# A macaron block on one core: other order of loads and first steps, scatters in four parts, gates by four 64 by 64 products, new places for the recurrence's work

## The reference

```python
x = x + 0.5 * ffn(layernorm(x))      # mixture of 8 experts, top 1
x = x + recurrence(layernorm(x))     # 3 layers over time, width 64
x = x + 0.5 * ffn(layernorm(x))      # same weights as the first

def ffn(x):                          # per token
    p = softmax(x @ Wr + br); e = argmax(p)
    h = relu(affine(layernorm(x)) @ W1[e] + b1[e])        # 256 -> 1024
    return (h @ W2[e] + b2[e]) * max(p)                   # 1024 -> 256

def layer(x):                        # width 64, x begins as h @ down_w.T
    xc = conv_b + sum(shifted(x, k) * conv_w[:, k] for k in range(4))
    r, i = sigmoid(xc @ Wr.T + br), sigmoid(xc @ Wi.T + bi)
    a = exp(8 * r * log_sigmoid(log_a))
    h[t] = a[t] * h[t - 1] + sqrt(1 - a * a)[t] * (i * xc)[t]
    return rms_norm(h @ out_w.T) * norm_w   # up_w takes it back to 256
```

## Time and profile before

| | |
|---|---|
| median of 3 runs | 768.86 us (766.00 to 772.32) |
| profiled execution, its own time | 763.67 us |
| its span, first to last instruction | 761.9 us |
| mean granted clock of TensorE | 0.930 |
| PE, DVE, ACT, POOL busy, share of the span | 90%, 54%, 35%, 23% |
| 16 DMA engines | 166 GB/s over the span |

### The profile page before, as it was taken

How to read it: one execution, slowest core, us unless ns; L and a number is a source line. 1 busy time by engine, 2 the same in 40 slices (tenths; PEclk the granted TensorE clock), 3 DMA queues, 4 the chain that set the end, 5 groups by cost and what they waited for, 6 DMA issues and landing times.

```text
span 761.9 us, 15311 instructions
## 1 busy us (share of the span) xinstructions
PE 684.7 (90%) x4350; PEld 594.2 (78%) x4350; DVE 410.7 (54%) x1427; ACT 264.3 (35%) x630; POOL 172.7 (23%) x178
## 2 busy tenths in 40 slices
PE   5548889899999999998997798989999889999993
PEld 4437679899988877887775686878888789999992
DVE  6466356333346576856877585865667332333331
ACT  3123112322334557343644454432522223222230
POOL 4622551111121120251212511240124111111111
PEclk9557899999999999999996898998999999999997
DMA  8989453665564444255253305353536464454440
GB/s 259 279 289 379 154 195 105 234 201 203 180 218 138 158 164 138 78 184 199 73 177 105 113 15 208 126 183 110 180 99 220 155 199 148 139 197 133 159 136 13
DMA packets 59919, 126.51 MB, mean 166 GB/s; under 512 B 8105, under 2 KB 36660, under 8 KB 59700
## 3 DMA queue, kind: packets, MB, share of 16 engines
q1 hardware_dynamic: 53204, 108.50, 43.7%
q0 software_dynamic: 6624, 16.92, 6.0%
HBM read 106.36 MB, written 20.35 MB: 166 GB/s over the span
## 4 chain that ended last, share of the span: by engine, by line
PE 80%; issue 6%; DVE 6%; ACT 2%; another core or an unknown queue 2%; DVEq 2%; DMA 1%; POOL 0%; SPq 0%; ACTq 0%; POOLq 0%
PE bank L1631 33%; PE bank L1645 33%; PE bank L1546 2%; PE bank L1618 2%; PE bank L1486 2%; PE bank L1551 1%; DVE st L717 1%; PE bank L1556 1%; PE bank L1538 1%; PE bank L1566 1%; PE bank L1577 1%; PE bank L1501 1%; PE bank L1514 1%; DMA rows<-in_L_attn_h 1%
## 5 line engine op out<-in xcount | busy, mean ns | idle before, releaser
L1645 PE MATMUL bank<-w,act_t 128*128 x1184 | 287.0, 393 | 9.3 <-issue 7.7
L1631 PE MATMUL bank<-mn_t,w 128*128 128x128 f32 x2368 | 287.3, 278 | 3.9 <-issue 3.9
L1631 PEld LDWEIGHTS bank<-mn_t,w 128*128 128x128 f32 x2368 | 278.7, 195 | 10.5 <-issue 10.2
L1645 PEld LDWEIGHTS bank<-w,act_t 128*128 128x128 f32 x1184 | 225.6, 197 | 48.9 <-issue 20.0
L1136 DVE TENSOR_SCALAR act_t<-bank,vec 128x128 f32<-128x128 f32 x296 | 83.5, 344 | 122.2 <-PE bank L1631 101.0
L1367 ACT ACTIVATE mn_t<-bank,vec 128x128 f32<-128x128 f32 x152 | 61.4, 454 | 230.3 <-PE bank L1618 215.2
L1377 ACT ACTIVATE act_t<-bank,vec 128x128 f32<-128x128 f32 x296 | 85.0, 368 | 105.8 <-PE bank L1631 76.5
L1143 DVE TENSOR_TENSOR y_b<-bank,b_all 128x256 f32<-128x256 f32 x74 | 31.4, 424 | 119.9 <-PE bank L1645 105.2
L625 POOL DMA_INDIRECT out_x<-res,pay x37 | 36.4, 984 | 243.4 <-DVE res L1149 242.8
L625 POOL DMA_INDIRECT x_middle<-res,pay x37 | 39.7, 1074 | 216.9 <-DVE res L1149 215.5
L616 POOL DMA_INDIRECT routed_rows<-rows,dest x64 | 63.5, 992 | 51.9 <-DVE dest L817 34.5
(11 more groups left out here) (211 smaller groups left out, 456.6 us busy)
## 6 DMA issues: line engine op xcount, KB each, us to landing
w<-in_L_ffn_W SPq DMA_DIRECT2D x82, 1024.0 KB
pay<-routed_rows SPq DMA_DIRECT2D x78, 130.0 KB, 2.1
rows<-in_L_attn_h SPq DMA_DIRECT2D x8, 512.0 KB, 6.9
rows<-x_middle SPq DMA_DIRECT2D x8, 512.0 KB, 5.1
routed_rows<-fill SPq DMA_DIRECT2D x2, 1040.0 KB, 10.7
b_all<-in_L_ffn_b SPq DMA_DIRECT2D x1, 1024.0 KB
routed_rows<-rows,dest POOLq DMA_INDIRECT x64
x_middle<-res,pay POOLq DMA_INDIRECT x37, 3.2
```

The source lines that it names most:

```text
L1631: last = t.matmul(b_hid[half][:, c % 4 * P:(c % 4 + 1) * P], w1[i % W1S][:, k * F + c * P:k * F + (c + 1) * P], mn_t[p][i % 2][:, k * P:(k ...
L1645: last = t.matmul(b_out[i % 2], act_t[i % 2][:, c * P:(c + 1) * P], w2[:, ds(eb * (WE // FC) + c * D, D)], start=c == 0, stop=c == FC - 1)
```

## The change

It does seven things. SP's queue: chunk 0, router weights, chunk 1, router bias, four `w2`, chunks 2 and 3, the parameters; after `s_tab` the first `w1`, a `w2` by use, the rows, and so on, and last the fill. The wait for the fill moves from the scatters to SP, ahead of the loads of the rows of the later parts. The first chunks' order on PE and ACT is changed: `ranks` of chunk 0 stands between the two transposes of chunk 1, and the exponentials between two keeps. `centre_down` goes ahead of the last table part, and the moments of chunk 3 go into slot 0. A chunk's 8 scatters stand at four positions, two at each, instead of two with four at each. The gates are four products of 64 by 64 weights, with one signal at the end: the input gate's go to bank 1 with the two sequences swapped, the other gate's to bank 0 unswapped, so that each of the four takes rows and columns of the array of its own; ACT's tanh of the input gate becomes two activations of 64 partitions that swap back. And nearly all positions are new. Cut to its core (the first hunk shows only the constants of which the text speaks):

```diff
@@ the positions (line 22 on) @@
...
-LN_TRANSPOSE = [[3984, 4032], [5065, 5089], [6576, 6624], [8065, 8089]]
...
-RESCALE = [[1009, 1278, 1681, 2065], [1152, 1416, 1827, 2260], [1275, 1608, 2040, 2424]]
-TAP = [[1034, 1279, 1705, 2065], [1176, 1416, 1922, 2281], [1276, 1610, 2041, 2426]]
-CONVOLVE = [[1032, 1296, 1705, 2112], [1153, 1464, 1829, 2280], [1277, 1632, 2042, 2472]]
-GATES = [[4224, 5232, 6960, 8544], [4776, 5952, 7680, 9264], [5160, 6625, 8256, 10032]]
...
-SCAN = [[1104, 1369, 1800, 2209], [1248, 1560, 1970, 2376], [1320, 1728, 2136, 2544]]
-PROJECT = [[4512, 5544, 7248, 9024], [5064, 6336, 8064, 9624], [5376, 7008, 8592, 10320]]
-SQUARES = [[1128, 1370, 1920, 2256], [1272, 1608, 2016, 2424], [1322, 1753, 2161, 2592]]
-NORMS = [[4560, 5569, 7250, 9072], [5088, 6384, 8088, 9672], [5424, 7104, 8640, 10368]]
...
-R_CHOOSE = [[None, None, 1, 120], [1417, 1872, 2304, 2736]]
...
-R_PLACE = [[None, None, 72, 192], [1488, 1969, 2352, 2784]]
...
-R_MOMENTS = [[1392, 1393], [1824, 1828], [2257, 2259], [2616, 2688]]
-R_SCATTER = [[[None, None], [None, None], [24, 25], [96, 97]], [[744, 745], [1008, 1009], [1176, 1177], [1392,
-    1393]]]
-TABLE_PARTS = [[[None, None, None, None, None, None], [217, 240, 264, 336, 337, None]], [[1514, 1609, 1658, 1659,
-    1660, 1704], [2041, 2064, 2066, 2067, 2137, 2138], [2400, 2425, 2473, 2474, 2475, 2520], [2809, 2832, 2833,
-    2834, 2835, None]]]
-LAYER_COLUMNS = 0
...
+LN_TRANSPOSE = [[3984, 4032], [5089, 5113], [6720, 6816], [8329, 8353]]
...
+RESCALE = [[1032, 1299, 1731, 2281], [1153, 1440, 1872, 2451], [1297, 1560, 2090, 2689]]
+TAP = [[1034, 1320, 1752, 2281], [1176, 1440, 1922, 2472], [1277, 1562, 2117, 2712]]
+CONVOLVE = [[1033, 1300, 1733, 2304], [1176, 1442, 1968, 2520], [1298, 1584, 2092, 2736]]
+GATES = [[4248, 5328, 7008, 9264], [4800, 5832, 7896, 10176], [5232, 6432, 8448, 11040]]
...
+SCAN = [[1104, 1392, 1800, 2400], [1248, 1512, 2064, 2592], [1416, 1728, 2208, 2808]]
+PROJECT = [[4560, 5664, 7248, 9720], [5088, 6144, 8328, 10488], [5713, 6913, 8904, 11328]]
+SQUARES = [[1128, 1416, 1920, 2424], [1272, 1536, 2112, 2640], [1418, 1753, 2232, 2832]]
+NORMS = [[4608, 5712, 7369, 9768], [5112, 6192, 8352, 10536], [5737, 7009, 9048, 11376]]
...
+R_CHOOSE = [[None, None, 48, 168], [1536, 1969, 2352, 2904]]
...
+R_PLACE = [[None, None, 72, 192], [1561, 2040, 2424, 2952]]
...
+R_MOMENTS = [[[None, None], [None, None], [None, None], [0, 1]], [[1464, 1489], [1824, 1825], [2305, 2306], [2857,
+    2880]]]
+R_SCATTER = [[[None, None, None, None], [None, None, None, None], [25, 48, 49, 72], [96, 97, 98, 120]], [[768, 792,
+    793, 794], [1008, 1032, 1033, 1034], [1200, 1224, 1225, 1226], [1464, 1488, 1489, 1490]]]
+TABLE_PARTS = [[[None, None, None, None, None, None], [217, 240, 312, 336, 337, None]], [[1608, 1632, 1730, 1732,
+    1734, 1752], [2066, 2089, 2091, 2093, 2094, 2112], [2450, 2472, 2473, 2474, 2521, 2544], [2977, 3000, 3001,
+    3002, 3003, None]]]
+LAYER_COLUMNS = 49
...
@@ -474,6 +476,9 @@
                     s = FIRST[p].index(i)
+                    if (p, s) != (0, 0):
+
+                        sp.wait_ge(s_fill[p], 16)
                     sp.wait_ge(s_tab, tables_at(p, s))
@@ -538,29 +543,29 @@
+            load_x(0, 0)
             sp.dma_start(wr[:, :].rearrange("p (k e) -> p k e", k=KD),
                          router_w.rearrange("(k p) e -> p k e", p=P)).then_inc(s_rt, 16)
-            sp.dma_start(rb_all[:, :], router_b[None, :].to_broadcast([P, E])).then_inc(s_rt, 16)
-            load_x(0, 0)
             load_x(0, 1)
-            sp.wait_ge(s_c2, 1)
-            empty_rows(0)
+            sp.dma_start(rb_all[:, :], router_b[None, :].to_broadcast([P, E])).then_inc(s_rb, 16)
+            for e in range(EAGER):
+                second_weights(e)
             load_x(0, 2)
-            second_weights(0)
+            load_x(0, 3)
             load_parameters()
-            load_x(0, 3)
-            for e in range(1, EAGER):
-                second_weights(e)
+
...
             slot_weights(0, 0)
+            sp.wait_ge(s_order, 1)
+            second_weights_by_use(0)
             for i in range(RING - 1):
                 next_rows(0, i)
-            sp.wait_ge(s_order, 1)
             for i in range(1, W1S):
-                second_weights_by_use(i - 1)
                 slot_weights(0, i)
-            for k in range(W1S - 1, LATER):
+                second_weights_by_use(i)
+            for k in range(W1S, LATER):
                 second_weights_by_use(k)
+            empty_rows(0)
...
@@ -607,12 +612,11 @@
-            def route(f, c, b):
+            def route(f, c, part):
...
                 pool.wait_ge(s_ds[f], c + 1)
-                pool.wait_ge(s_fill[f], 16)
-                for j in range(TPC):
-                    t = (b * NC + c) * TPC + j
+                for k in range(2 * part, 2 * part + 2):
+                    t = (k // TPC * NC + c) * TPC + k % TPC
                     g.indirect_dma_start(
@@ -636,9 +640,9 @@
                                 powers(m, c)
-                            for b in range(NB):
-                                if k == R_SCATTER[f][c][b]:
-                                    route(f, c, b)
+                            for part in range(NJ // 2):
+                                if k == R_SCATTER[f][c][part]:
+                                    route(f, c, part)
...
@@ -678,8 +682,8 @@
             for c in range(HC):
-                for b in range(NB):
-                    route(0, c, b)
+                for part in range(NJ // 2):
+                    route(0, c, part)
             first_pass()
@@ -743,7 +747,7 @@
             def centre_router():
-                dve.wait_ge(s_rt, 32)
+                dve.wait_ge(s_rt, 16)
                 dve.wait_ge(s_wrc, 1)
@@ -763,6 +767,7 @@
                     v.memset(seen, 0.0)
+                    dve.wait_ge(s_rb, 16)
                 m, rs = mv[0][cc], inv_std[0][cc]
@@ -1091,8 +1096,9 @@
                                 add_recurrence(c, part)
-                            if k == R_MOMENTS[c][part]:
-                                moments(R2, c, part)
+                            for f, m in ((0, R1), (1, R2)):
+                                if k == R_MOMENTS[f][c][part]:
+                                    moments(m, c, part)
                         if k == LN_WIDE[c]:
@@ -1236,11 +1242,10 @@
             order_of_use()
+            centre_down()
             tables(0, 0, 5)
-            centre_down()
-            for c in range(HC, NC):
-                for b in range(NB):
-                    moments(R1, c, b)
+            for b in range(NB):
+                moments(R1, 2, b)
             norm(0, 0)
@@ -1311,8 +1316,13 @@
                 cc = c % 2
-                act.wait_ge(r_g[c % 2], 2 * turn(l, c))
-                a.activation(r_ti_b[cc], bk[cc][1][:, :], ACT.Tanh, scale=0.5, bias=unit(l, U_IB)).then_inc(r_t[c % 2], 1)
+                act.wait_ge(r_g[c % 2], turn(l, c))
+                for b in range(NB):
+
+                    o = NB - 1 - b
+                    last = a.activation(r_ti_b[cc][b * DO:(b + 1) * DO, :], bk[cc][1][o * DO:(o + 1) * DO, :], ACT.Tanh,
+                                        scale=0.5, bias=unit(l, U_IB)[o * DO:(o + 1) * DO, :])
+                last.then_inc(r_t[c % 2], 1)
                 a.activation(r_a_b[cc], bk[cc][0][:, :], ACT.Tanh, scale=0.5, bias=unit(l, U_RB))
@@ -1428,13 +1438,13 @@
             keep_logits(R1, 0)
-            for part in range(2):
-                keep(R1, 1, part)
+            keep(R1, 1, 0)
             exponentials(0, 0)
+            keep(R1, 1, 1)
             keep_logits(R1, 1)
-            for part in range(2):
-                keep(R1, 2, part)
+            keep(R1, 2, 0)
             exponentials(0, 1)
+            keep(R1, 2, 1)
             keep_logits(R1, 2)
@@ -1487,7 +1497,7 @@
             def router_sums():
-                pe.wait_ge(s_rt, 32)
+                pe.wait_ge(s_rt, 16)
                 for k in range(KD):
@@ -1540,10 +1550,14 @@
                 pe.wait_ge(r_xc[c % 2], turn(l, c))
-                for m in range(2):
-                    o = (m * NL + l) * P
-                    t.matmul(bk[c % 2][m][:, :], rec_t[:, o:o + P], r_x_b[c % 2], start=True, stop=True).then_inc(r_g[c % 2], 1)
+                for m, b in ((1, 0), (1, 1), (0, 0), (0, 1)):
+                    o = (m * NL + l) * P + b * DO
+                    to = (b + m) % NB
+                    last = t.matmul(bk[c % 2][m][to * DO:(to + 1) * DO, :], rec_t[b * DO:(b + 1) * DO, o:o + DO],
+                                    r_x_b[c % 2][b * DO:(b + 1) * DO, :], start=True, stop=True)
+                last.then_inc(r_g[c % 2], 1)
...
@@ -1740,10 +1754,10 @@
             turn_logits(0, 0)
-            for part in range(2):
-                transposes(R1, 1, part)
+            transposes(R1, 1, 0)
+            ranks(0, 0)
+            transposes(R1, 1, 1)
             logits(R1, 1)
```

(1 more changed line is left out.)

## The result

The changed kernel takes 758.34 us (median of 7 runs, 756.07 to 765.79), the kernel before 769.32 us beside it (7 runs, 766.00 to 772.32). The ratio is 0.9891, 95% interval 0.9858 to 0.9923: 1.1% faster, where 5% was forecast, and the time is 1.3 us above the range. The profiled execution of the changed kernel took 756.07 us, 7.6 less than that of before (763.67), where the sum said 39.

What follows compares the result with a forecast made beforehand. PE sets the time: 74 slots of 7.25 us are 536 us, plus other work and waits. Terms -25 - 8 - 3 - 7 + 4 = -39 gave 725 profiled, 730 median; forecast 721 to 741, range 716 to 757.

Steps and rivals of the forecast that it cites:

- A series of 6 ends 2 x 1.3 = 2.6 us earlier: Scatter series on POOL: six instead of eight end sooner, shortening five pauses of PE by 2.6 us each as one bound.
- the part on the scatters: Six stretches with scatter series lose 32.1 us; splitting each series was to gain 25 us, bounds 20 and 32.
- the pauses do not depend on the length of the series: Rival on POOL's scatters: issuing 64 at all is what matters, so the 25 us stay: 755; chance 0.17.
- Gates: Recurrence gates on PE: four small products side by side take 1.06 to 1.2 us, not 1.88; 8 us less over twelve.
- hidden by the slots' products except between the passes: ACT's extra tanh at the gates lengthens each chain by 0.69 us, which PE's slot work was to cover elsewhere.
- Ahead of the first slot: Start of the kernel: moving chunk 3's moments off DVE's list there was to gain 3 us; bounds 8 gained, 5 lost.
- The fill ... nothing, unless PE waits for that: Load order at the start: 1 MB moved from ahead of the first slot to ahead of the fourth `w1` costs nothing.
- Between the passes: Moving convolution, gates and choice behind the second pass's first slots brings DVE's norm earlier: gain 7 us, bounds 0 and 10.
- New waits: Closer steps in the new order, at places 36 to 64, make PE, DVE and ACT wait: 4 us loss, bounds 0 and 12.
- just in time: Chunk 3's last six scatters at place 62: rows loadable from about 63.5 and 1 MB of `w1` still arrive for their slot.

Runs made afterwards that it cites:

- the last run: Changed kernel at the earlier kernel's places with spread scatters, with only the filler load moved back to early: 726.66 us, 0.9486 of the kernel before.

## Why the prediction was wrong

**The step that failed** is "A series of 6 ends 2 x 1.3 = 2.6 us earlier", in the part on the scatters, with its 25 us. There was no series of six. I read the places of POOL's list as times, though the first scatter of a series waits for its destinations (1.79 us in the earlier trace rows, 2.98 in the changed kernel): what stands behind a waiting instruction is due when the wait ends, and a store and six scatters were. The store was not counted either; six scatters and a store would have been a row of seven, which still cost 1.96 us in a quiet slot. The measured term is +3.6 us (50.3 against 46.7), and one gap alone, which makes the split real, gave 21 us in the changed kernel and 25 in the kernel before. So the price of the pause was read about rightly, and the change did not touch it. With the gap the changed kernel takes 739.19 us, 9 above the forecast of 730; the gates, which gave next to nothing, are most of that.

**The rival** "the pauses do not depend on the length of the series" named the time (755) for a wrong reason: the runs with added series show that they do, with nothing lost at five in a row and 7 us at ten. The case that came, a change that doesn't do what it says, was not among the rivals.

**Gates.** The mechanism was right and the size near (0.5 us a turn in the slots, forecast 0.7), the four products ran side by side as forecast (1.09 us a set), and the time did not follow: 0 to 2 us of the 8. What failed, as far as the runs show it, is that the longer chain of ACT was to be "hidden by the slots' products except between the passes": with the new gates one slot at the old places takes 4.4 us more.

By the Trainium skill, TensorEngine Tiling (Array Packing), section Restrictions and Gotchas, different row tiles cannot access one PSUM bank at the same time. Here two products with different rows of the array write one bank in different partitions, and the set of four takes 1.09 us, little over one product (0.97 us, half of the 1.93 of a set that uses two quarters twice); the measurement decides against that reading.

**Ahead of the first slot**, -3 forecast, +0.5 in the first pair of profiles, but -2.2 in the mean of eleven and five: right in sign and near in size. What I did not ask is what the pause would do to DVE, once chunk 1's scatters meet DVE ahead of its tables instead of among them. And the gain does not reach the end: with the start at 55.4 us the time stayed the same. "The fill ... nothing, unless PE waits for that" was wrong too: DVE waits for rows behind it, and moving the fill alone gave 7 us in the last run. Its cost in the changed kernel lies in the first of the five stretches and so in the +3.6.

**Between the passes**, -7 forecast, -7.4 measured: right in place and size.

**New waits**, +4 forecast: what it said of chunk 3 ("just in time") was too kind. The last scatters at place 62 run into the stage start, 12.1 us lost there against 8.4. With the row broken the new places still take 38.7 us there against 31.5, so it is the lateness of chunk 3 and not only the row. Spreading this row further was not tried.

The terms as measured in the profiled executions: scatters, filler and the late chunk 3 together +3.6, gates -6, start +0.5, between the passes -7.4, sum -9.3 against -7.6; the rest of 1.7 us is not assigned. They are differences between stretches and not what each part of the change is worth: the gates' 6 us of products are there, and yet taking them back costs the kernel only 1 to 2 us.

## What to carry to other kernels

Break up rows of indirect DMAs on POOL, and count the stores in: up to five in a row cost PE nothing in the quiet slots here (one of five in a busy slot 4 us), ten cost it 7 to 9 us, and one break of 3 us was enough; but keep the breaks few and short, or stores and the loads behind them come late. An entry's place in an engine's list is not its time: behind a wait everything that is due piles up and goes out in one row. A load that nobody awaits still delays those that somebody does, if it is put among them when the queues are full.

## What the runs showed of the hardware

During an unbroken row of indirect DMAs on POOL, ACT or DVE or both stand still from some microseconds into it until about when it ends, or up to 3 us longer (2.73 us in a row of four, 4.33 in one of five, 10.31 in one of nine, 16.63 in one of thirteen). PE runs dry later: in quiet slots nothing was lost to rows of up to five, 0.86 us to six, 1.96 to seven, 6.98 to ten, with one row of six that cost nothing. It depends on the number of DMAs or on the time that they take, not on their bytes (rows of 64 bytes: 8.29 us) or rows (16 of them: 6.47 us). POOL's being busy is not enough: beside 24 us of other POOL operations ACT and DVE went on until the rows were late.

The Trainium skill, DMA: Bandwidth & Descriptors, section SWDGE vs HWDGE vs iDMA, names one software path for all DMAs issued from GpSimd, direct and indirect. Whether plain ones stop the engines too, no run here shows: the eight that were tried took POOL 4.35 us in all.

What stops the engines stays open. The 16 instructions of a slot's second products ran on at full speed in the row shown above (3.62 us from 599.10), while DVE and ACT stood; later ones came in ones and twos with gaps. No run took an engine's waits or its instruction supply apart.
